# Reordered beginning, passage and tiles of an attention-and-FFN kernel, with twelve products of zeros while the first inputs load

## The reference, cut to what matters

```python
q = layernorm(x)                                  # over the 512 positions
qh = softmax(Wq @ q, over the 64 rows of a head) * 64**-0.5      # 8 heads x 64
kh = softmax(Wk @ ctx, over the 512 positions)
vh = Wv @ ctx
context = einsum('bhdn,bhen->bhde', kh, vh)
out = Wo @ einsum('bhde,bhdn->bhen', context, qh) + bo
x = x + out / max(norm(out, axis=1), 1e-12) * g * 64**0.5
# FFN on 2048 rows of 512
z = layernorm(x)
inter = z @ c1_w.T @ c2_w.T                       # rank 16, then 1792 columns
idx = argmax in each block of 32 columns          # 56 blocks
h = relu(w1[idx] . z);  x = x + h @ w2t[idx]
```

## Time and profile before

| what | value |
|---|---|
| median of 3 runs | 789.4 us (789.12 to 789.5) |
| the profiled execution: its time | 789.44 us |
| its span, first to last instruction | 787.6 us |
| mean granted TensorE clock | 0.989 |
| busy: PE, DVE, ACT, POOL | 755.1, 611.2, 404.1, 475.4 us |
| `turn_h(1)` of tile 0 starts | 407.19 us |

### The profile page before, as it was taken

How to read it: one execution, slowest core, us unless ns; L and a number is a source line. 1 busy time by engine, 2 the same in 40 slices (tenths; PEclk the granted TensorE clock), 3 DMA queues, 4 the chain that set the end, 5 groups by cost and what they waited for, 6 DMA issues and landing times.

```text
span 787.6 us, 13635 instructions
## 1 busy us (share of the span) xinstructions
PE 755.1 (96%) x4768; PEld 549.5 (70%) x4768; DVE 611.2 (78%) x938; ACT 404.1 (51%) x802; POOL 475.4 (60%) x546
## 2 busy tenths in 40 slices
PE   4999999999999999999879999999999999999998
PEld 3566566656665666566557887778877788877786
DVE  6899999999999999999457666776567765677653
ACT  3899999999999999998311111111111111111111
POOL 2899999988888899865244324543335543355431
PEclk9999999999999999999899999999999999999999
DMA  5333433333233333211001001111011110111000
GB/s 144 101 105 102 128 103 103 104 97 98 82 89 98 98 109 91 75 48 48 7 21 41 21 20 41 41 41 39 2 41 41 41 40 1 42 41 41 27 15 14
DMA packets 30388, 48.04 MB, mean 61 GB/s; under 512 B 4721, under 2 KB 13553, under 8 KB 30321
## 3 DMA queue, kind: packets, MB, share of 16 engines
q1 hardware_dynamic: 29648, 46.19, 20.2%
q10 hardware_dynamic: 672, 0.98, 0.5%
HBM read 38.77 MB, written 8.39 MB: 60 GB/s over the span
## 4 chain that ended last, share of the span: by engine, by line
PE 36%; issue 30%; POOL 21%; DVE 10%; ACT 2%; DMA 1%; DVEq 0%; POOLq 0%; SPq 0%; ACTq 0%
PE po L1015 9%; PE turn L1000 5%; PE turn L983 5%; POOL Q L406 5%; PE slot L1041 4%; PE slot L1055 4%; POOL E L321 4%; POOL E L330 3%; PE po L930 2%; POOL weights_lo L362 2%; PE slot L902 2%; DVE E L515 2%; PE po L1026 2%; POOL c_low L396 1%; POOL x_low L352 1%
## 5 line engine op out<-in xcount | busy, mean ns | idle before, releaser
L321 POOL TENSOR_TENSOR E<-E,rank 128x256 bf16<-128x256 bf16 (+1 forms) x64 | 66.6, 1040 | 182.2 <-DVE E L490 182.2
L406 POOL TENSOR_TENSOR Q<-Q,qrec 128x1024 f32<-128x1024 f32 x64 | 121.3, 1903 | 41.7 <-DVE qrec L621 41.3
L1015 PE MATMUL po<-E,ctxT 128*64 128x512 f32 x256 | 117.1, 600 | 0.0
L1018 PE MATMUL po<-QT,G 128*64 128x512 f32 x256 | 116.7, 599 | 0.0
L727 ACT ACTIVATE wk_hi<-turn 128x256 fp32r<-128x256 f32 (+1 forms) x32 | 15.7, 491 | 171.5 <-PE turn L915 171.5
L902 PE MATMUL slot<-weights_hi,c_high 128*128 128x512 f32 (+1 forms) x256 | 97.9, 382 | 2.1 <-DVE c_low L472 2.1
L902 PE MATMUL slot<-weights_hi,c_low 128*128 128x512 f32 (+1 forms) x256 | 95.6, 373 | 0.0
L902 PE MATMUL slot<-weights_lo,c_high 128*128 128x512 f32 (+1 forms) x256 | 95.3, 372 | 0.0
L760 ACT ACTIVATE E<-slot,neg_kmax 128x512 f32<-128x512 f32 x128 | 86.2, 685 | 11.1 <-DVE neg_kmax L607 11.0
L930 PE MATMUL po<-weights_hi,x_high 128*128 128x512 f32 x224 | 88.2, 394 | 0.0
L573 DVE TENSOR_REDUCE qmax<-slot 128x16 f32<-128x1024 f32 x64 | 75.3, 1218 | 14.8 <-PE slot L1055 14.7
(11 more groups left out here) (115 smaller groups left out, 1711.4 us busy)
## 6 DMA issues: line engine op xcount, KB each, us to landing
c_in<-in_ctx SPq DMA_DIRECT2D x64, 128.0 KB, 2.6
x_in<-in_x SPq DMA_DIRECT2D x64, 128.0 KB, 2.6
stage<-in_ffn_w SPq DMA_DIRECT2D x32, 225.0 KB, 2.6
attn_out<-po_sb SPq DMA_DIRECT2D x32, 128.0 KB, 2.2
ctxT<-in_ctxT SPq DMA_DIRECT2D x31, 128.0 KB, 2.2
attn<-attn_out SPq DMA_DIRECT2D x8, 256.0 KB, 2.9
x<-in_x SPq DMA_DIRECT2D x8, 256.0 KB, 2.7
E<-attn_out SPq DMA_DIRECT2D x8, 256.0 KB, 2.9
```

The costliest lines, as they stand in the source:

```text
L321: nc.gpsimd.tensor_tensor(ranked[c % 2][:, 0:w], mask[c % 2][:, 0:w], rank[:, 0:w], ALU.mult).then_inc(i_ranked, 1)
L406: nc.gpsimd.tensor_tensor(half, half, qrec[1 - par][:, s, :].unsqueeze(2).broadcast_to([P, HALF, D]), ALU.mult).then_inc(q_scaled, 1)
L1015: nc.tensor.matmul(po[0:C, :], ctxT[1 - par][:, m, :], E[1 - par][:, :, m * P:(m + 1) * P], start=(m == 0), stop=(m == NT - 1)).then_inc(p ...
L1018: nc.tensor.matmul(po[C:P, :], G[:, m, :], QT[m][:], start=(m == 0), stop=(m == HT - 1)).then_inc(out_mm, 1)
```

## The change

Beginning: `wqk` is loaded as two DMAs with a semaphore each, `wv` and `woT` on SyncE's queue behind x(0), `bo` and `ctxT` on ScalarE's behind its two first roundings. The split of wq goes to ScalarE (high part) and GpSimd (rest, ahead of `bias(0,0)`). VectorE's `max_k(1)` goes behind `split_first_x` and `statistics(1,1)`; `shift_q(0)` goes ahead of `max_q(1)` in step 0; the copy of vo goes to ScalarE. `statistics(2,0)` goes from step 0 into step 1 ahead of `max_q(0)`, and `statistics(3,1)` behind `gains` of step 1; GpSimd's biases and ScalarE's `norm_x` of step 1 move accordingly. `turn_e` of step 0 uses banks 0, 1, 2, 0. TensorE begins with twelve 128x128 products of a zeroed piece of `QT[0]`, into `turn[2]`, whose result is not used.

Passage: `xT_rest(0,0)` goes behind `sum_q(31,1)` and its reciprocal, `xT_round(0,0)` ahead of `po_copy`, `turn_attn(1)` and `square(1)` from step 33 into step 32, `project(0,0,2)` out of tile 0 into step 32.

Tiles: VectorE does `first_max(1)`, `gate(0)` and then `result_of` and `scale`; `h_low(0)` goes ahead of `residual`; TensorE's `turn_back(p+1)` goes behind `hide(p,2)`.

```diff
...
 
         inter, hidden = ([s[:, i, :] for i in range(2)] for s in slot)
         turned, acc, pre = turn[0:2], po, turn[2]
-        bank_e = lambda g, m: turn[(8 * g + (0, 1, 4, 7)[m]) % 3]
+        bank_e = lambda g, m: turn[(0, 1, 2, 0)[m] if isinstance(g, int) and g == 0 else (8 * g + (0, 1, 4, 7)[m]) % 3]
         bank_q = lambda g, m: turn[(8 * g + (2, 3, 5, 6)[m]) % 3]
 
         attn_loaded, xr_loaded = ([sem(f"{n}{i}") for i in range(2)] for n in ("attn_loaded", "xr_loaded"))
...
 
                 load_c(0)
                 load_x(0, 0, 0)
+                sp.dma_start(wv, A["wv"]).then_inc(vo_in, 16)
+                sp.dma_start(woT, A["woT"]).then_inc(vo_in, 16)
                 load_x(1, 0, 1)
                 load_stage(0)
                 sp.wait_ge(c_ready, 1)
...
                                                 ALU.subtract).then_inc(c_ready, 1)
                     split_items()
                     if known == -1:
+                        pool.wait_ge(wq_hi_done, 1)
+                        nc.gpsimd.tensor_tensor(wq_lo[:], w_raw[:, 0, :], wq_hi[:].bitcast(fp32),
+                                                ALU.subtract).then_inc(wq_lo_done, 1)
                         bias(0, 0)
+                    if known == 0:
+                        bias(1, 1)
                     if real(known, -1):
 
                         for s in range(2):
...
                             nc.gpsimd.tensor_tensor(
                                 half, half, qrec[1 - par][:, s, :].unsqueeze(2).broadcast_to([P, HALF, D]),
                                 ALU.mult).then_inc(q_scaled, 1)
-                    bias(g + 2, par)
+                    if known == 1:
+                        bias(2, 0)
+                    if known > 0:
+                        bias(g + 2, par)
                     if known == B - 2:
                         invert(0)
                     if known == B - 1:
...
 
             @block.vector
             def _(dve):
-                def split_weights(n, hi, lo):
-                    nc.vector.tensor_copy(hi[:], w_raw[:, n, :]).then_inc(w_hi, 1)
-                    dve.wait_ge(w_hi, 2 - n)
-                    nc.vector.tensor_tensor(lo[:], w_raw[:, n, :], hi[:].bitcast(fp32),
-                                            ALU.subtract).then_inc(w_lo, 1)
-
-                def copy_vo():
-                    dve.wait_ge(vo_mm, 1)
-                    nc.vector.tensor_copy(vo[:], po[0:C, :].rearrange("c (h o) -> c h o", h=HEADS))\
-                        .then_inc(vo_ready, 1)
+                def split_wk():
+                    dve.wait_ge(wk_in, 16)
+                    nc.vector.tensor_copy(wk_hi[:], w_raw[:, 1, :]).then_inc(wk_hi_done, 1)
+                    dve.wait_ge(wk_hi_done, 1)
+                    nc.vector.tensor_tensor(wk_lo[:], w_raw[:, 1, :], wk_hi[:].bitcast(fp32),
+                                            ALU.subtract).then_inc(wk_lo_done, 1)
 
                 def norms(a):
                     dve.wait_ge(squared, a + 1)
...
                     if not last:
                         norms(p + 1)
                     block_max(p, 2)
+                    first_max(1)
+                    gate(0)
                     if p:
                         result_of(p - 1, 1 - par)
-                    first_max(1)
                     if not last:
                         scale(p + 1)
-                    gate(0)
                     block_max(p, 3)
                     first_max(2)
                     gate(1)
+                    h_low(0)
                     if not last:
                         residual(p + 1, 1 - par)
-                    h_low(0)
                     gate(2)
                     if not last:
                         normalize(p + 1, 1 - par)
...
                             nc.vector.reciprocal(qrec[1 - par][:, s, :], qsum[:, s, :]).then_inc(q_rec, 1)
 
                     if known == -1:
-                        dve.wait_ge(w_in, 16)
-                        split_weights(1, wk_hi, wk_lo)
+                        nc.vector.memset(QT[0][:, 0:P], 0.0).then_inc(idle_set, 1)
+                        split_wk()
                         dve.wait_ge(c_hi, 1)
                         nc.vector.tensor_tensor(c_low[0][:], c_in[:], c_high[0][:].bitcast(fp32),
                                                 ALU.subtract).then_inc(c_ready, 1)
-                        split_weights(0, wq_hi, wq_lo)
                         statistics(0, 0)
                     if known == 2:
                         dve.wait_ge(consts_in, 16)
                         nc.vector.tensor_scalar(gain8[:], gain8[:], float(C) ** 0.5, None, ALU.mult).then_inc(gain_done, 1)
                     max_k(0)
                     invert_q(0)
-                    max_k(1)
                     if known == 0:
                         split_first_x()
-                        copy_vo()
                         statistics(1, 1)
-                        dve.wait_ge(x_moments, 2)
-                        dve.wait_ge(x_biased, 1)
-                    if known == B:
-                        xT_rest(0, 0)
+                    max_k(1)
                     sum_q(g - 1, 1 - par, 1)
                     if real(known, -1):
                         dve.wait_ge(k_exped, 2 * g)
                         nc.vector.reciprocal(krec[:], ksum[1 - par][:]).then_inc(k_rec, 1)
                     invert_q(1)
-                    if known > 0:
+                    if known == B:
+                        xT_rest(0, 0)
+                    if known == 1:
+                        statistics(2, 0)
+                        dve.wait_ge(x_moments, 3)
+                        dve.wait_ge(x_biased, 2)
+                    elif known > 1:
                         statistics(g + 2, par)
                     if known == B - 2:
                         norms(0)
                     if known == B - 1:
                         residual(0, 0)
                     max_q(0)
+                    if known == 0:
+                        shift_q(0)
                     max_q(1)
-                    shift_q(0)
-                    if known == 0:
-                        statistics(2, 0)
+                    if known > 0:
+                        shift_q(0)
                     if known == B - 1:
                         normalize(0, 0)
                     shift_q(1)
                     gains()
+                    if known == 1:
+                        statistics(3, 1)
                     if known == B - 2:
                         scale(0)
                     sum_q(g, par, 0)
...
 
             @block.scalar
             def _(act):
-                nc.scalar.dma_start(w_raw, A["wqk"]).then_inc(w_in, 16)
+                nc.scalar.dma_start(w_raw[:, 1, :], A["wqk"][:, 1, :]).then_inc(wk_in, 16)
+                nc.scalar.dma_start(w_raw[:, 0, :], A["wqk"][:, 0, :]).then_inc(wq_in, 16)
                 nc.scalar.dma_start(ident[:], A["ident"]).then_inc(rest_in, 16)
-                nc.scalar.dma_start(wv, A["wv"]).then_inc(vo_in, 16)
-                nc.scalar.dma_start(woT, A["woT"]).then_inc(vo_in, 16)
-                act.wait_ge(powers_set, 3)
-                nc.scalar.dma_start(po_bias[C:P, :], A["bo"]).then_inc(rest_in, 16)
-                nc.scalar.dma_start(ctxT[0][:], A["ctxT"][0]).then_inc(ctxT_loaded[0], 16)
 
                 def square(a, bank):
                     act.wait_ge(attn_turned, a + 1)
...
 
                 def step(g, k, par, known):
                     if known == 1:
-                        act.wait_ge(w_lo, 2)
+                        act.wait_ge(wk_lo_done, 1)
+                        act.wait_ge(wq_lo_done, 1)
+
+                    def copy_vo():
+                        act.wait_ge(vo_mm, 1)
+                        nc.scalar.activation(vo[:], po[0:C, :].rearrange("c (h o) -> c h o", h=HEADS),
+                                             ACT.Copy).then_inc(vo_ready, 1)
 
                     def exp_q(s):
                         if real(known, 0):
...
                     if known == -1:
                         act.wait_ge(c_loaded, 32)
                         nc.scalar.activation(c_high[0][:], c_in[:], ACT.Copy).then_inc(c_hi, 1)
+                        act.wait_ge(wq_in, 16)
+                        nc.scalar.activation(wq_hi[:], w_raw[:, 0, :], ACT.Copy).then_inc(wq_hi_done, 1)
+                        act.wait_ge(powers_set, 3)
+                        nc.scalar.dma_start(po_bias[C:P, :], A["bo"]).then_inc(rest_in, 16)
+                        nc.scalar.dma_start(ctxT[0][:], A["ctxT"][0]).then_inc(ctxT_loaded[0], 16)
                         return
                     exp_k(0)
                     exp_k(1)
-                    if known > 0:
+                    if known == B:
+                        xT_round(0, 0)
+                    if known == 0:
+                        copy_vo()
+                    else:
                         po_copy()
+                    if known > 1:
```

(30 more changed lines are left out.)

## The result

| | before | after |
|---|---|---|
| median, same chip | 789.26 us (787.26 to 789.5, 4 runs) | 771.16 us (770.72 to 772.01, 4 runs) |
| ratio, 95% interval | | 0.9777 [0.9759, 0.9796] |
| profiled execution: time, span | 789.44, 787.6 us | 771.59, 769.8 us |
| last keys of the batch loop start | 363.89 us | 368.30 us (+4.41) |
| `turn_h(1)` of tile 0 starts | 407.19 us | 400.18 us (passage -11.42) |

The kernel is 18.1 us faster; 771.3 was forecast. The three differences of the profile stand beside forecasts of +4.3, -11.5 and -10.9.

What follows compares the result with a forecast made beforehand. GpSimd was taken to pace batch steps 2 to 11, with TensorE stops in the passage and tiles. Terms -11.5 - 10.9 + 4.3 = -18.1 from 789.4 gave 771.3 us; own range 768.5 to 774.5, 8 in 10 for 766.5 to 777.

Steps and rivals of the forecast that it cites:

- Passage: Steps 31 to 33 into tile 0: TensorE's three stops go and the clock stays up, -11.5 us, bounds -6.9 and -12.
- rival 2: Passage gives its stops alone, as the clock falls in stretches of short transposes: 775.9 us, chance 0.12.
- the 4.65 us at half clock: Passage: half the time of TensorE's 6.01 and 3.30 us of work at clock 0.50 is lost.
- Tiles: Each tile: an earlier `gate(0)` lets `turn_h(0)` start 0.78 us earlier, 14 times, -10.9 us, bounds -8.5 and -10.9.
- Rivals 3 and 4: Tiles: 3, `gate(1)` holds TensorE, no gain, 782.2 us, chance 0.05; 4, late `normalize` delays `turn_x`, 806, chance 0.02.
- Beginning: Steps 0 to 2: nothing saved, and late `statistics(3,1)` delays GpSimd to the end, +4.3 us, bounds +2.5 and +6.
- rival 1: Batch loop: GpSimd's late start costs nothing, through slack or a far earlier `gains`: 767.0 us, chance 0.15.
- The step that failed: Steps 2 to 11: TensorE waits for `Q` in step 2, its clock may fall, but being faster it makes that up.
- Zeros: Kernel start: twelve products take 3.8 us, hidden before the keys; a clock kept up would save some 0.7, not taken.
- `bo`: Beginning: issued at some 6.7, lands at 9.8 to 12.3, or 8.7 by the skill; cost 0 to +0.3 us.

Runs made afterwards that it cites:

- e5: The kernel before with the passage and tile edits, its own beginning kept: 765.72 us, ratio 0.9696.
- e6: The kernel after with both statistics back in their old places, `norm_x` behind `po_copy` and `bias(2,0)` in step 0: 766.65 us, ratio 0.9704.
- e8: The kernel after with SyncE issuing the tiles' load of x ahead of the store of the result: 771.78 us, ratio 0.9765.
- e7: The kernel after with `statistics(3,1)` alone moved back ahead of `max_q(0)` in step 1: 769.93 us, ratio 0.9748.
- e9: The kernel after with 24 products of zeros in place of twelve: 773.03 us, ratio 0.9785.
- e3: The kernel before with the edits of the beginning alone, zeros among them: 794.94 us, ratio 1.0071.
- e4: The kernel after without the twelve products of zeros and the zeroing: 772.7 us, ratio 0.9781.
- e10: The kernel before with passage and tile edits, plus the tiles' load of x issued ahead of the store: 767.59 us, ratio 0.9704.

## Why the prediction was right, step by step

**Passage: right in each step.** Forecast -11.5, seen -11.42, and -11.43 alone. All in the time of after, which runs 4.4 later up to there: `xT_round` starts at 381.52 (377.26 + 4.4 = 381.7), `xT_rest` at 383.12 (378.8 + 4.4 = 383.2), `hide(0,0,0)` at 384.52 (380.2 + 4.4 = 384.6), `turn_h(0)` at 396.74 (392 + 4.4 = 396.4). The clock stayed at 1.00, so rival 2 is out: the 4.65 us at half clock went with the stops.

**Tiles: right in sum, with two terms off.** `turn_h(0)` does start without a wait in each tile. But a tile is 0.85 shorter, not 0.78: 14 x 0.85 = 11.9, outside the bounds given (-8.5 and -10.9). I had taken the distance of a transpose from the product ahead of it (0.23); the tile also gets back 0.07 elsewhere, which I didn't trace. On the other side stands a dependency that the prediction missed. It said of `result_of`, "comes 1 us later and `down(0)` needs it 7 us after that: nothing". It looked for TensorE's need alone; SyncE's queue waits for the same semaphore, and the load behind it feeds `residual`. That gave back 0.43 + 0.37 + 0.51 = 1.3 us in this profile. -11.9 + 1.3 = -10.6, and -10.84 was seen; the rest is in the ends of the row of tiles. That the sum hit -10.9 is luck: the two misses nearly cancel. Rivals 3 and 4 are out: from 412 to 740 us no wait of TensorE is left in the summary of waits, so neither `gate(1)` nor `turn_x` holds it.

**Beginning: the mechanism and the size are right.** GpSimd's longest wait behind `x_low` of step 1 is 3.42 us, for `statistics(3,1)`, which ended at 32.82, forecast 33.15; `x_low` of step 2 is at 34.22, forecast 34.55, and step 3 at 45.70, forecast 46.1. It goes on whole to the end, since the nine steps before were dense: rival 1 is out, by e5 and e6. The stop of `turn_q(0)` in step 2 was forecast as a wait for `Q`; it is 4.25 us.

**The step that failed**: "where its clock may fall; it is the faster of the two in steps 2 to 11 and makes that up". It doesn't. TensorE comes out of the stop at half the clock (`turn_q(0)` takes 1.97 us, 1.04 in the passage), and in step 3 GpSimd's scaling waits for `qrec`, the reciprocals of VectorE's sums. Between the two stand the keys of step 3, for which `max_k(0)` waits ahead of the reciprocal: 1.71 us in e8, 0.34 in after, and in e6, which has no stop, not at all. This chain is read from the timelines; no run changes it alone. The price is 0.3 to 0.4 us with 3.4 us at half clock (after 11.91, e7 11.91; e9 11.79), and 1.5 to 1.8 us with 6.8 us (e3 13.04, e4 13.14, e8 13.29), over 11.50. In the forecast's sum GpSimd was 0.33 early and step 3 to 4 0.4 long, so it came out at +4.4 for +4.3: luck again, as with 6.8 us at half clock the profile of after would have been over 1 us longer. In the medians the beginning costs more, 5.4 (6.4 by the ratios) and 5.5.

**Zeros.** Their price was put at 0.32 us each and 3.8 in all, bounds 2.5 and 5.1; twelve took 4.32 to 5.49 in seven profiles, so the upper bound was too low: in after one took 0.46 us, nearly three times the 0.16 of a 64-column product and not twice. The end at 6.54 left 0.26 us to the keys, and the cover was nearly gone. Their use was put at "some 0.7", and not taken, for TensorE's idling between the queries. The idling of 2.44 us is there, and the clock was at 0.50 from 13.5 to 20.3. But the keys at full clock brought 0.68 all the same where the idling behind the zeros was short, up to `x_low` of step 1; that it lasts to the end of the kernel is not shown.

**`bo`** was issued at 5.40 and landed 3.6 us later, at 9.0, ahead of `queries(0)` at 10.77: no cost, in the range of the earlier trace rows. The Trainium skill, "DMA: Bandwidth & Descriptors", "Anatomy of one DMA", has its 2 us of fixed cost for loads that GpSimd issues, and `bo` is on ScalarE's queue; carried over as an estimate it would be there at 7.4. The measured 3.6 decides.

**Left open.** Why the split of c(0) begins at 6.05 in one run and 0.5 to 1.0 us later in others of the same queue order (the keys start at 6.80, 7.30, 7.41, 7.48 and 7.76 in after, e8, e4, e7 and e3). Why the stretch at half clock behind equal stops is 3.4 or 6.8 us long. What the loads, banks and splits of the new beginning do, each by itself. And whether e10 is slower than e5: their ranges overlap, and the edit can't act before the tiles. In e5's profile the first queries, at 13.75, already take 0.50 us a pair, at full clock; in e10's the first queries, at 13.82, and the next keys, at 22.22, take 0.80, and the queries at 29.26 are the first to take 0.50. That goes with `x_low` of step 2 at 29.09 and 31.63. What sets it was not tried.

## What to carry to other kernels

When an operation is moved, follow every waiter of its semaphore, the DMA queues above all: a load issued behind a store that waits for the moved result is moved too. When one engine is dense over many steps, what makes its first dense step late is paid in full at the end, whatever was freed elsewhere; here undoing that piece of the reordering, the two statistics and what hangs on them, was worth a quarter of the whole gain (4.5 of 18.1 us by the medians). And test the parts of a change alone: a sum of the right size held one part that made the kernel slower.

## What was unexpected in the hardware

Five profiles (after, e3, e4, e8, e9) have the same stop of TensorE in step 2, 4.25 to 4.27 us, and after it the clock was at 0.50 for 3.4 us in two and for 6.8 us in three. The difference is worth 1.1 to 1.5 us at the end of the kernel, by the intervals from step 3 to step 4. A stop of 2.17 us (e7) was followed by 3.4 us at 0.50.

The transposes and small products of the passage, with no stop over 1.1 us between them, ran at 1.00 as the large ones did (365 to 401 us in after). And the length of a row of small products at the start of the kernel isn't fixed: the same twelve took 4.32 us in e3 and 5.49 in after. The windows of after, then of e3, show why:

```profile
3.00:4.00 1.00, 1.00 (x7) 1.00 (x7) 0.67 (x2) 0.40 (x1) 0.00 (x0) 1.00 0.93 325
4.00:5.00 1.00, 1.00 (x6) 1.00 (x6) 0.45 (x1) 0.00 (x0) 0.00 (x0) 1.00 1.11 267
...
3.00:4.00 1.00, 1.00 (x7) 1.00 (x7) 0.00 (x0) 0.40 (x1) 0.00 (x0) 1.00 1.02 260
4.00:5.00 1.00, 1.00 (x11) 1.00 (x11) 0.70 (x2) 0.00 (x0) 0.00 (x0) 1.00 1.11 255
```

From 4 to 5 us TensorE has 11 records in e3 and still 6 in after (and 12 from 6 to 7 in e9): from about 4 us on e3's zeros ran at full speed, after's not before their end. The clock printed beside them is 1.00 in both, so at the start of the kernel it can't be relied on.
